# TensorE's semaphores in the edge layers of a graph network: raised by a drain behind the last product instead of by the product

## The reference

```python
x = _layernorm(x + _L0_gnn_ref(x, edge_index, ...), axis=-1)   # attention, 8 heads
x = _layernorm(x + _L1_gnn_ref(x, src, dst, edge_type_32, edge_weight1, ...), axis=-1)   # 32 relations, 8 bases
x = _layernorm(x + _L2_gnn_ref(x, src, dst, ...), axis=-1)   # two attention convolutions
x = _layernorm(x + _L3_gnn_ref(x, edge_index, edge_weight, node_vec, ...), axis=-1)   # attention and a state-space scan
```

```python
e = leaky_relu(el[src] + er[dst], 0.2)
ex = exp(e - segment_max(e, dst)[dst])
a = ex / segment_sum(ex, dst)[dst]
rst = segment_sum(feat[src] * a[..., None], dst)
```

## Time and profile before

| what | us |
|---|---|
| median of 3 runs | 10313.51 |
| lowest and highest | 10280.58, 10322.89 |
| the profiled execution's own time | 10205.21 |
| its span, first to last instruction | 10203.4 |
| granted TensorE clock over the span, share of full speed | 0.689 |

### The profile page before, as it was taken

How to read it: one execution, slowest core, us unless ns; L and a number is a source line. 1 busy time by engine, 2 the same in 40 slices (tenths; PEclk the granted TensorE clock), 3 DMA queues, 4 the chain that set the end, 5 groups by cost and what they waited for, 6 DMA issues and landing times. The chain is left out here.

```text
span 10203.4 us, 95759 instructions
## 1 busy us (share of the span) xinstructions
PE 4723.2 (46%) x18992; PEld 3701.4 (36%) x18993; DVE 4940.6 (48%) x11530; ACT 1260.0 (12%) x2760; POOL 5284.4 (52%) x4989
## 2 busy tenths in 40 slices
PE   3172444444666665444455433333343445444534
PEld 3022333333555554333333332323233334343423
DVE  8525777774323333333333233333344656566644
ACT  1020111111000110000000000000011222222211
POOL 0215666665666675655555455556654465545310
PEclk6576677666777777666666666666666777667767
DMA  1113554542222221222222222222222222222100
GB/s 65 35 33 95 152 149 136 154 130 80 75 74 69 77 76 52 66 71 63 62 76 64 54 62 73 70 66 77 69 65 68 75 84 77 83 80 78 57 28 7
DMA packets 485807, 772.79 MB, mean 76 GB/s; under 512 B 296063, under 2 KB 316342, under 8 KB 482011
## 3 DMA queue, kind: packets, MB, share of 16 engines
q0 software_dynamic: 265536, 666.90, 23.5%
q10 hardware_dynamic: 19838, 70.21, 1.8%
q1 hardware_dynamic: 200345, 34.81, 1.8%
HBM read 822.37 MB, written 46.03 MB: 85 GB/s over the span
## 5 line engine op out<-in xcount | busy, mean ns | idle before, releaser
L848 POOL DMA_INDIRECT gat_rows<-scratch_gat,gat_index x1856 | 1858.1, 1001 | 1131.3 <-issue 560.1
L1726 POOL DMA_INDIRECT m_rows<-scratch_gat,m_index x928 | 1125.7, 1213 | 1063.6 <-DVE m_work L2016 523.7
L1125 PE MATMUL gat_ps<-gat_work,k_ident 128*128 128x256 f32 x3712 | 1150.9, 482 | 1098.3 <-DVE gat_work L919 718.0
L1125 PEld LDWEIGHTS gat_ps<-gat_work,k_ident 128*128 128x128 f32 x3712 | 909.2, 250 | 1359.8 <-issue 1011.6
L1270 POOL DMA_INDIRECT rel_rows<-scratch_x,rel_index x928 | 1011.7, 1090 | 482.3 <-issue 323.8
L848 POOL DMA_INDIRECT conv_rows<-scratch_kv,conv_index x928 | 932.7, 1005 | 555.3 <-issue 277.8
L1125 PE MATMUL conv_ps<-conv_work,k_ident 128*128 128x256 f32 x1856 | 670.2, 539 | 1013.5 <-DVE conv_work L919 759.1
L1125 PEld LDWEIGHTS conv_ps<-conv_work,k_ident 128*128 128x128 f32 x1856 | 513.1, 284 | 1171.0 <-issue 1023.2
L919 DVE TENSOR_TENSOR gat_work<-gat_rows,gat_psprob 128x2048 f32<-128x2048 f32 x232 | 530.6, 2287 | 796.4 <-ACT gat_psprob L1060 725.9
L1524 PE MATMUL rel_ps<-rel_factor,rel_rows 128*128 128x128 f32 x3712 | 604.0, 330 | 207.1 <-issue 127.0
L1524 PEld LDWEIGHTS rel_ps<-rel_factor,rel_rows 128*128 128x128 f32 x3712 | 572.4, 243 | 221.3 <-issue 158.6
(11 more groups left out here) (457 smaller groups left out, 8038.1 us busy)
## 6 DMA issues: line engine op xcount, KB each, us to landing
m_bc<-scratch_bc ACTq DMA_DIRECT2D x25, 2048.0 KB
gat_rows<-scratch_gat,gat_index POOLq DMA_INDIRECT x1856
conv_rows<-scratch_kv,conv_index POOLq DMA_INDIRECT x928
rel_rows<-scratch_x,rel_index POOLq DMA_INDIRECT x928
m_rows<-scratch_gat,m_index POOLq DMA_INDIRECT x928
scratch_runs<-e_runs_sb SPq DMA_DIRECT2D x1, 12890.6 KB
scratch_kv<-p_row ACTq DMA_DIRECT2D x25, 256.0 KB
gat_index<-scratch_slots SPq DMA_DIRECT2D x232, 4.0 KB
```

Of the source, the lines that this page charges most:

```text
L848: pool.indirect_dma_start(out=rows[b][:, s, :], out_offset=None, in_=table, in_offset=bass.IndirectOffsetOnAxis(ap=index[b][:, s:s + 1], a ...
L1125: ins = pe.matmul(ps_sum[min(b, 1)], ident, work[b][:, s, :], start=s == 0, stop=s == S - 1)
L1726: pool.indirect_dma_start(out=rows[b][:, s, :], out_offset=None, in_=dr["gat3"], in_offset=bass.IndirectOffsetOnAxis(ap=index[b][:, s:s + ...
```

## The change

In the five edge layers each `then_inc` on the last product or transpose of a group is replaced by a drain of PE behind it that raises the same semaphore. The products, their order, all waits and all other engines are as before. `build_slots`, `count_edges` and `join` keep the old form. All places look like these:

```diff
 def sum_slots(w, a, b):
                 for s in range(S):
                     ins = pe.matmul(ps_sum[min(b, 1)], ident, work[b][:, s, :], start=s == 0, stop=s == S - 1)
-                ins.then_inc(summed, 1)
+                pe.drain().then_inc(summed, 1)
...
                 elif layer == "gat1":
                     pe.wait_ge(new_x, 2 * t + 2)
-                    transposed(pe, ps_h, hid, ident).then_inc(turned, 1)
+                    transposed(pe, ps_h, hid, ident)
+                    pe.drain().then_inc(turned, 1)
                     pe.wait_ge(xt_ready, 2 * t + 2)
                     product(pe, ps[1][:, 0:F], ht, wt["wb1b"], start=False)
-                    product(pe, ps[2][:, 0:wide], ht, wt["fc2"]).then_inc(made, 1)
+                    product(pe, ps[2][:, 0:wide], ht, wt["fc2"])
+                    pe.drain().then_inc(made, 1)
...
-                ins.then_inc(record_turned, 1)
+                pe.drain().then_inc(record_turned, 1)
...
-                ins.then_inc(hot_turned, 1)
+                pe.drain().then_inc(hot_turned, 1)
...
-                ins.then_inc(weights_made, 1)
+                pe.drain().then_inc(weights_made, 1)
...
-                ins.then_inc(released[b], 1)
+                pe.drain().then_inc(released[b], 1)
...
                 if h == 1:
-                    ins.then_inc(summed, 1)
+                    pe.drain().then_inc(summed, 1)
```

More of the change, by code:

```diff
@@ L1537, in apply_bases @@
                 if h == 1:
-                    ins.then_inc(summed, 1)
+                    pe.drain().then_inc(summed, 1)
             def finish_tile(t):
                 pe.wait_ge(new_x, t + 1)
-                transposed(pe, ps_t, cur, ident).then_inc(turned, 1)
+                transposed(pe, ps_t, cur, ident)
+                pe.drain().then_inc(turned, 1)
                 pe.wait_ge(xt_ready, t + 1)
-                product(pe, ps_end[:, 0:wide], xt, fc1).then_inc(made, 1)
+                product(pe, ps_end[:, 0:wide], xt, fc1)
+                pe.drain().then_inc(made, 1)
             def pair(w, a, t=None, before=None):
@@ L1742, in project @@
                 pe.wait_ge(sems["rows"], t * 16 + 16)
-                transposed(pe, ps_t, xs, kp["ident"][:]).then_inc(sems["turned"], 1)
+                transposed(pe, ps_t, xs, kp["ident"][:])
+                pe.drain().then_inc(sems["turned"], 1)
                 pe.wait_ge(sems["xt"], t + 1)
@@ L1748, in project @@
                                         stop=k == 1)
-                ins.then_inc(sems["xz"], 1)
+                pe.drain().then_inc(sems["xz"], 1)
             def front(t):
@@ L1755, in front @@
                     ins = pe.matmul(ps_d, w_x[:, k, :], src[:, k * P:(k + 1) * P], start=k == 0, stop=k == 1)
-                ins.then_inc(sems["dbc"], 1)
+                pe.drain().then_inc(sems["dbc"], 1)
                 pe.wait_ge(sems["dbc_out"], t + 1)
@@ L1759, in front @@
                     ins = pe.matmul(ps_dt[:, k, :], w_dt[:, k * P:(k + 1) * P], dbc[0:R, :], start=True, stop=True)
-                ins.then_inc(sems["dt"], 1)
+                pe.drain().then_inc(sems["dt"], 1)
             def sum_states(t):
@@ L1766, in sum_states @@
                         ins = pe.matmul(ps_y[:, k, :], kp["ident"][:], hs[:, k, n, :], start=n == 0, stop=n == NS - 1)
-                    ins.then_inc(sems["sums"], 1)
+                    pe.drain().then_inc(sems["sums"], 1)
             def flow_out(t):
@@ L1773, in flow_out @@
                     ins = pe.matmul(ps_o, y[:, k, :], w_out[:, k, :], start=k == 0, stop=k == 1)
-                ins.then_inc(sems["made"], 1)
+                pe.drain().then_inc(sems["made"], 1)
             def sum_slots(w, j, b):
```

12 lines of the change are left out of this document (8 added, 4 removed).

## The result

| what | us |
|---|---|
| changed kernel, median of 4 runs | 10485.34 (10476.44 to 10505.55) |
| before, same comparison, median of 4 runs | 10309.02 |
| ratio | 1.0177, 95% interval 1.015 to 1.0205 |
| the profiled execution of the changed kernel, its span | 10493.69, 10491.9 |

The change makes the kernel slower by 176 us, 1.8%. The forecast was 52 us: the sign was right, the time lies in the range, the loss is 3.4 times the forecast. The two profiled executions lie 288 us apart, 112 more than the medians: the one of before, 10205.21 us, is none of the four of the table and is 75 us shorter than the shortest of them, and its chip is not known.

The account below looks back on a forecast made before the run. No engine is full; POOL's gathers come nearest to a bound, with TensorE's completions held during their runs. Lateness 26 + restart 26 + hold 0 = 52 us on the 10313.5 us median gave about 10370 us; range 10,220 to 10,640.

Parts of the forecast that it names:

- The bound and the hold: Edge layers: TensorE's instructions cannot retire during long runs of POOL's gathers, giving 1900 us of waits "until remote".
- a drain that goes past the hold: Rival at the held waits: drains see products end despite the hold, some 800 us faster, 9500 us; chance 0.25.
- One sign to look for: Trace of the changed kernel: PE's drains behind L562 in a long run of gathers last 10 to 20 us.
- The quiet price: Cost of drains outside holds: 26 us for the semaphore's own lateness plus 26 us for the restart.
- the semaphore's lateness: Drains somebody waits for at once: 520 of 1175, each raising its semaphore 0.05 us later, 26 us.
- the restart: Relation layer: next weight load bare behind a drain, 0.3 us each; a third counted, 26 us, bounds 0 and 78.
- Behaviour in a hold: Drains in held runs: each ends when the product's message would have come, so 0 us; upper bound 173.
- the drain takes PE's run-ahead: Rival in gat1, gat2, relation layer, scan: next products start after the hold, 370 us slower, 10,680 us; chance 0.15.
- The upper bound for the hold: Edge layers: drains in holds paced like other instructions, 0.7 us each for 21% of 1175, 173 us.
- Hidden drains: Rival: POOL and DVE cover the restart, sums' drains cost nothing; 0 to 45 us, 10315 to 10360; chance 0.32.
- the upper bounds: High end of the range: 59 lateness, 78 restart and 173 hold, together 310 us, put at 10,640 us.

Follow-up runs that it names:

- e1_bare: Kernel before, products still raising their semaphores, plus a drain that raises nothing behind each at all 1175 places: 10273.44 us against 10179.01, ratio 1.0092.
- e10_change: Changed kernel, unedited, on a chip without holds: 8561.26 us against 8539.84 for the kernel before, ratio 1.0019.
- e8_half_drain: Changed kernel with POOL gathering 4 of 8 slots per chunk, chip without holds: 7776.49 us; the same with products raising semaphores took 7582.88.
- e4_ends: Kernel before with the change's drains only at gat1's and gat2's tile ends and in the scan's steps (325): 10196.78 us against 10179.01, ratio 1.0023.
- e17_change: Changed kernel, unedited, on a chip with holds: 10303.10 us against 10199.02 for the kernel before, ratio 1.0111.
- e3_rel: Kernel before with the change's drains only in the relation layer (386): 10242.96 us against 10179.01, ratio 1.0058.
- e2_sums: Kernel before with the change's drains only behind the 464 sums of slots in the four attention layers: 10220.68 us against 10179.01, ratio 1.0044.
- e15_half_drain: Changed kernel with POOL gathering 4 of 8 slots per chunk, chip with holds: 8220.80 us; the same with products raising semaphores took 8114.27.
- e19_rel_released: Kernel before with a drain only behind the relation layer's 116 chunk sums, on a chip without holds: 8549.65 us against 8545.64, ratio 1.0004.
- e9_before: Kernel before, unedited, traced on a chip without holds: 8538.15 us against 8539.84 for the same kernel, ratio 0.9999.
- e5_change: Changed kernel, unedited, on a chip without holds: 8559.01 us against 8537.75 for the kernel before, ratio 1.0024.

## Why the prediction was right and wrong

**The bound and the hold: right.** The waits of the earlier trace rows kept their length or grew a little and changed their name from "remote" to PEq, the drain behind L562 came no earlier, and PE's busy time hardly moved (4785.8 us for 4723.2). The reading of the earlier trace rows, that it is the completion of instructions which is held and not the message, is confirmed by drains of 20.93 us in a run of gathers and by e1_bare. The rival of a drain that goes past the hold, given 0.25, is out.

**One sign to look for failed.** The prediction wanted the drains behind L562 to last 10 to 20 us. Those of gat1's second half last 0.43 to 0.69 us; the long one is the sum's drain ahead of them, in which L562 waits its turn.

**The quiet price: too high.** The two terms of 26 us, the semaphore's lateness and the restart, make 52; the chips without holds measured 21. For the lateness the sum took 0.05 us; in e10_change the median drain ends 0.02 us behind the modelled end of its products. The prediction let the 464 sums cost nothing and took a third of the relation layer's restart, since POOL covers the rest. Without holds that layer lost 18 us. e8_half_drain took POOL's cover away and found 133 us in that layer, more than the upper bound of 78 that the prediction had for its restart: it had counted 260 of that layer's 386 drains, and the 0.3 us for each came to 0.34, lateness included.

**The failed step is "Behaviour in a hold", where the sum took 0.** It argued that the drain ends when the product's message would have come, which is true. It left out what stands behind the drain, though it named it: the waits and weight loads of PE's next group, which had run ahead in the hold and now start after it. Where nothing is held the change costs 21 us, twice; on chips with holds 104 and 176 us, and the bare drains 94. So holds are most of the loss, 104 - 21 = 83 us on one chip and 176 - 21 = 155 us on the first, where the sum had 0. This subtraction takes the quiet price for equal on both kinds, which is not shown.

**Where that arises is shown, by which path in part.** The relation layer has 66 to 78 us of it in the traces of e1_bare to e4_ends and 66 in e17_change, for 18 without holds. There the held drains behind the weights keep a ready chunk sum for 152 us (e3_rel), and POOL, which waits for the chunk sums, waits 102 us longer (166.9 in e3_rel, 65.2 in e2_sums). But in e3_rel 22 of those 43 waits of POOL, 83 us, have no held drain at the chunk sum or right ahead of it. A rival stands there that no run settled: the restart, of which the prediction took a third for POOL's cover. In the kernel before POOL stands still for 280 of 1615 us of this layer where there are holds and for 102 of 1392 where there are none, so that it may cover less of the restart, and e15_half_drain lost 96 us in this layer with few drains held. e19_rel_released was to tell the two apart and met a chip without holds. In gat1 and gat2 the drains keep L562's transposes for over 500 us and next to nothing comes of it. From the one tile above, with 0.94 us from the hold's end to L1091, 50 tile ends would be 47 us, an estimate; the windows have 4 to 29 us, and 10 in e17_change. The 42 us of e2_sums can't be put into layers, since no trace of the kernel before is from its chip.

**The mechanism had been written down as a rival** ("the drain takes PE's run-ahead") with 0.15, and priced at 370 us, 3.7 us in 100 tiles. The price was a whole sum of slots for each tile. In the tile above someone waits only for the short group, 0.38 us of transposes with their restart, while the sum behind it is wanted a chunk later; the windows of gat1 and gat2 fit that, with 4 to 29 us where the rival had 185 for these two. The upper bound for the hold, 173 us, worked out from pacing at 0.7 us for each drain, came near the 155 by chance: the drains of e3_rel aren't paced by 0.7 us each, 35 of 65 behind L1512 aren't late and one is by 8.6 us.

**Hidden drains** (the rival called "same", 0.32) is what happens where nothing is held: +0.2%. One slip of arithmetic changes nothing: the upper bounds, 310 us above the median, give 10,624 us, and the range was closed at 10,640.

**No price per drain.** A drain cost 0.018 us with POOL as cover and without holds, 0.08 to 0.15 us with holds (0.17 for the 386 of the relation layer alone), and 0.34 us in a relation layer without cover. The Trainium skill (PSUM — Partial Sum Buffer, Engine vs sequencer instructions) puts the increment on the matmul as a matter of correctness, and speaks of no price. In time, too, it was the better place on each chip: no run had the drained form faster.

## What to carry to other kernels

When a semaphore comes late, ask first whether the engine is still executing behind it: work then runs ahead while the message is late, and a drain, which stops the sequencer, puts that work after the wait. Price an added drain by what stands behind it on its own engine, by who waits for that and by what covers it there, not by its duration: 500 us of transposes kept back cost at most 29 us here, 152 us of kept chunk sums came with a loss of 66 to 78. A trace of the kernel before from the same chip is what tells a layer's loss from a chip's. And where a wait ends for no reason that the profile shows, end the thing that goes on beside it (here POOL's runs of gathers, by a pause) before touching the engine that seems late: it showed that the long runs make the difference, and the pauses gained 2.2% on a chip with holds, while on one without they lost 17%.

## What the runs showed of the hardware

The kernels met two kinds of chips. In three comparisons the kernel before took 10,179, 10,199 and 10,309 us, and PE's completions were held in long runs of POOL's gathers, with waits of up to 28 us among those of the earlier trace rows and a drain of 31.5 us in the changed kernel. In three others, two of them on one chip, it took 8538, 8540 and 8546 us, without a wait until remote in the traces of e9_before, e5_change and e10_change or a drain held in a run, at the same 1.00 us for a gather. How long a run has to be, the changed kernel's first trace tells roughly (gathers less than 0.6 us apart counted as one run): of the drains whose products ended with up to 6 gathers of a run issued, 84 of 834 ended over 1 us late, with 7 to 9 of them 130 of 193, with 10 or more 136 of 159. In e5_change, with 7 or more, it was none of 860. A kernel whose runs of gathers end after 8 takes 9973 and 9978 us on the two kinds. What differs between the chips, and by which path POOL's gathers hold PE's completions, is open. With pauses some holds are left on such a chip (508 us of waits until remote, 18 in ACT's L1093 of up to 11.0 us). A second drain behind a first took 13 ns of PE's sequencer, and 0.03 us of the kernel's time.
